# A four-layer convolution kernel: the deformable stage's preparation and tiles, ordered by image in place of by pair of images

## The reference, cut to what matters

```python
x = x + _L1_conv_ref(_gn(x), ...)    # 3x3 convolution, 64 to 64 channels, with bias
x = x + _L2_conv_ref(_gn(x), ...)    # deformable 3x3 convolution
# _gn: each of 32 groups (2 neighbouring channels of one image) to mean 0 and variance 1
# deformable: from the normed image, for each pixel and each of 9 taps,
off  = _conv(x, offset_w, offset_b)                   # a (dy, dx)
mask = 2.0 * sigmoid(_conv(x, mod_w, mod_b))
# the image at the displaced point, from its 4 corners, bilinearly; then
sampled = (v00*(1-wy)*(1-wx) + v01*(1-wy)*wx + v10*wy*(1-wx) + v11*wy*wx) * mask
out = einsum('bkhwc,ock->bohw', sampled, w2)
```

## Time and profile before

| what | value |
|---|---|
| median of three runs | 6821.06 us (6818.94 to 6823.68) |
| the profiled execution | 6821.58 us, span 6819.7 us |
| POOL busy | 4754.8 us, 70% of the span |
| DVE busy | 5149.9 us, 76% |
| PE busy | 4541.4 us, 67% |
| ACT busy | 2515.4 us, 37% |

### The profile page before, as it was taken

The page is one execution under the profiler, slowest core; times in us unless marked ns, Lnnn a source line. Parts: engine busy times, 40 slices in busy tenths (PEclk is TensorE's granted clock), DMA queues, the critical chain, the costliest instruction groups (busy, mean ns, idle before and its releaser), DMA issues. The chain is left out here.

```text
span 6819.7 us, 55261 instructions
## 1 busy us (share of the span) xinstructions
PE 4541.4 (67%) x14990; PEld 2454.8 (36%) x14990; DVE 5149.9 (76%) x4038; ACT 2515.4 (37%) x3865; POOL 4754.8 (70%) x3364
## 2 busy tenths in 40 slices
PE   2755765576466546633325787878888787888887
PEld 1543552233323323422222343434333343443443
DVE  2855864367666766766655898989989898998998
ACT  0111110212111101200005565666666565666664
POOL 0744752277777777777754787878878787887887
PEclk8766777575566566555557999999999999999999
DMA  3533542334443543433323444444454444444443
GB/s 115 115 73 67 115 92 63 94 104 122 124 130 104 142 131 104 136 120 105 105 87 113 147 152 142 153 139 162 141 151 149 145 148 150 150 152 142 153 151 117
DMA packets 377421, 853.16 MB, mean 125 GB/s; under 512 B 194816, under 2 KB 237720, under 8 KB 372772
## 3 DMA queue, kind: packets, MB, share of 16 engines
q1 hardware_dynamic: 292420, 618.02, 30.6%
q0 software_dynamic: 84672, 231.32, 11.2%
HBM read 766.90 MB, written 56.48 MB: 121 GB/s over the span
## 5 line engine op out<-in xcount | busy, mean ns | idle before, releaser
L2016 POOL TENSOR_TENSOR ma_hc<-ma_h,ma_cc 128x784 f32<-128x784 f32 x1024 | 1885.7, 1849 | 631.9 <-DVE ma_h L1918 497.6
L797 POOL DMA_INDIRECT fl_quad<-table,fl_idx x1764 | 1694.5, 961 | 779.0 <-issue 536.7
L1573 PE MATMUL ma_bank<-ma_hc,ident 128*128 128x392 f32 x4096 | 1530.1, 496 | 76.2 <-POOL ma_hc L2016 76.2
L1918 DVE TENSOR_TENSOR_SCAN ma_h<-ma_da,ma_state,ma_bank 128x784 f32<-128x784 f32 x768 | 1417.5, 1846 | 165.6 <-POOL ma_hc L2016 67.6
L1791 ACT ACTIVATE ma_da<-ma_dt,ma_a_neg 128x784 f32<-128x784 f32 x1024 | 948.3, 943 | 496.3 <-DVE ma_h L1918 479.5
L952 DVE TENSOR_TENSOR fl_part<-fl_quad,fl_bank 128x2304 f32<-128x2304 f32 x196 | 500.5, 2554 | 741.2 <-DMA fl_quad<-table,fl_idx 740.9
L1906 DVE TENSOR_TENSOR ma_bank<-ma_dtu,ma_bank 128x784 f32<-128x784 f32 x1024 | 981.3, 958 | 38.3 <-PE ma_bank L1560 37.6
L1094 PE MATMUL fl_bank<-ident,fl_tap 128*128 128x128 f32 (+1 forms) x980 | 245.8, 414 | 989.7 <-DVE xres L969 929.1
L1573 PEld LDWEIGHTS ma_bank<-ma_hc,ident 128*128 128x128 f32 x4096 | 711.1, 191 | 506.5 <-POOL ma_hc L2016 80.2
L1560 PE MATMUL ma_bank<-ma_bc,ma_sel 96*128 96x512 bf16 (+1 forms) x2048 | 518.9, 335 | 442.4 <-DVE ma_h L1918 430.9
L960 DVE TENSOR_REDUCE fl_tap<-fl_part 128x576 f32<-128x2304 f32 x196 | 796.4, 4063 | 0.1
(11 more groups left out here) (217 smaller groups left out, 6166.2 us busy)
## 6 DMA issues: line engine op xcount, KB each, us to landing
ma_cc<-c_rows SPq DMA_DIRECT2D x512, 784.0 KB, 4.1
mx_win<-flat SPq DMA_DIRECT2D x64, 878.0 KB, 10.4
fl_quad<-table,fl_idx POOLq DMA_INDIRECT x1764, 2.7
table<-fl_xt SPq DMA_DIRECT2D x64, 392.0 KB
mx_mask<-in_c_mask SPq DMA_DIRECT2D x56, 294.0 KB, 4.3
ma_xs<-ma_x SPq DMA_DIRECT2D x64, 196.8 KB, 5.4
ma_xs<-ma_x SPq DMA_DIRECT2D x64, 196.5 KB, 5.8
mx_xf<-flat SPq DMA_DIRECT2D x8, 816.0 KB, 15.1
```

Of the source, the lines that this page charges most:

```text
L797: gp.indirect_dma_start(quad[i][:, kk, :], None, k["tables"][q], bass.IndirectOffsetOnAxis(ap=idx[i][:, kk:kk + 1], axis=0))\
L1573: ins = pe.matmul(ps_y[:, t, :], ident[:], hc[:, n % RH, at], start=False, stop=(n == DS - 1))
L1918: dve.tensor_tensor_scan(h[:, i % RH, :], da[:, i % RH, :], ps_bu[i % 2], before, ALU.mult, ALU.add).then_inc(scand, 1)
L2016: gp.tensor_tensor(hc[:, i % RH, :], h[:, i % RH, :], cc[:, i % (NGRP * GRP), :], ALU.mult)\
```

## The change

Preparation is split by image. `program` begins with the first norm of pair 0 (`add_up`, 4 steps) and 24 steps of preparation of image 0; then come the tiles of image b, each followed by one step of image b + 1, and in steps 19 to 22 of an even image the first norm of the next pair. The tiles of a pair are no longer in alternation: 24 of image 0, 24 of image 1, the shared last one. Each image has a second norm of its own (`measure`, `variance`, `factors` with e = 1 + h), so a pair has three in place of two, each still over all 128 partitions. `y` gets a buffer of its own. POOL waits for one table at each image, and an even image's gathers get the first half of the table. SP stores the tables in the new order. Cut to its core, with the indices of semaphores left out where they only follow the new count:

```diff
-        def program(prepare, tile):
-            for s in range(NSEQ):
-                prepare(0, s)
-            for q in range(NPAIR):
-                for s in range(NSEQ):
-                    tile(q, s, NSEQ * q + s)
-                    if q + 1 < NPAIR:
-                        prepare(q + 1, s)
+        def program(add_up, prepare, tile):
+            for s in range(4):
+                add_up(0, s)
+            for s in range(NF):
+                prepare(0, 0, s)
+            for b in range(NB):
+                q, h = b // 2, b % 2
+                for s in range(NF + h):
+                    tile(NSEQ * q + NF * h + s)
+                    if s < NF and b + 1 < NB:
+                        prepare((b + 1) // 2, 1 - h, s)
+                    if h == 0 and 19 <= s < 23 and q + 1 < NPAIR:
+                        add_up(q + 1, s - 19)
...
-        y = om[:, 0:PIX]
+        y = s_.sb("y", [P, PIX])
...
             def load_y(q):
                 if q:
-                    sp.wait_ge(oturned, START + 4 * q)
+                    sp.wait_ge(joined, START + q)
...
             store_table(0)
-            store_table(1)
             for q in range(NPAIR):
                 if q + 1 < NPAIR:
-                    prepare(q + 1)
+                    load_y(q + 1)
+                store_table(2 * q + 1)
+                if q + 1 < NPAIR:
+                    store_table(2 * q + 2)
                 sp.wait_ge(added, START + NSEQ * (q + 1))
...
-                if s == 0:
+                if T == 0:
                     gp.wait_ge(bordered, START + 256 * NPAIR)
-                    gp.wait_ge(tabled, START + TABD * (2 * q + 2))
+                if s % NF == 0 and s < LAST:
+                    gp.wait_ge(tabled, START + TABD * (2 * q + s // NF + 1))
...
+                table = k["tables"][q][0:TAB, :] if s < NF else k["tables"][q]
                 for kk in range(K2):
-                    gp.indirect_dma_start(quad[i][:, kk, :], None, k["tables"][q],
+                    gp.indirect_dma_start(quad[i][:, kk, :], None, table,
...
+                if e == 2:
+                    dve.wait_ge(added, START + NSEQ * q + 8)
                 for i in range(NSTAT):
                     dve.bn_stats(stats[:, i, :], xres[:, q, i * STAT:(i + 1) * STAT]).then_inc(moments, 1)
...
+            def add_up(q, s):
+                if s == 0:
+                    join(q)
                 if s == 1:
-                    join(q)
+                    measure(q, 0)
                 if s == 2:
-                    measure(q, 0)
+                    variance(3 * q)
                 if s == 3:
-                    variance(2 * q)
-                if s == 4:
                     factors(q, 0)
...
+            def prepare(q, h, s):
+                b = 2 * q + h
+                if s == 0:
+                    pad(q, 0, h)
+                if 2 <= s <= 8:
+                    grow(q, h, s - 2)
+                if s == 8:
+                    measure(q, 1 + h)
+                if s == 9:
+                    variance(3 * q + 1 + h)
+                if s == 10:
+                    factors(q, 1 + h)
+                    pad(q, 1, h)
+                if s == 16:
+                    place(b, 0)
+                if s == 17:
+                    place(b, 1)
+                    corner(q, h)
+                if s == 18:
+                    weigh(q, h)
...
+            def prepare(q, h, s):
+                if 1 <= s <= 7:
+                    conv(q, h, s - 1)
+                if s == 8:
+                    pair(3 * q + 1 + h)
+                if 11 <= s <= 14:
+                    offset(q, h, 2 * (s - 11))
+                    if s < 14:
+                        offset(q, h, 2 * (s - 11) + 1)
+                if 15 <= s <= 18:
+                    turn_x(q, h, s - 15)
+                if 15 <= s <= 16:
+                    turn_offsets(q, h, s - 15)
...
+            def prepare(q, h, s):
+                if s == 0:
+                    pad(q, 0, h)
+                if s == 8:
+                    square(3 * q + 1 + h)
+                if s == 9:
+                    root(q, 1 + h)
+                if s == 10:
+                    pad(q, 1, h)
+                if 11 <= s <= 14:
+                    take_offsets(q, h, 2 * (s - 11))
+                    if s < 14:
+                        take_offsets(q, h, 2 * (s - 11) + 1)
+                if 15 <= s <= 18:
+                    take_x(q, h, s - 15)
+                if s == 17:
+                    sigmoid(2 * q + h)
```

More of the change, by code:

```diff
@@ L672, in stage_flow @@
         hd2, var, lnv = (s_.sb(x, [P, 1]) for x in ("hd2", "var", "lnv"))
-        rstd = [s_.sb(f"rstd{i}", [P, NPAIR]) for i in range(2)]
-        nmr = [s_.sb(f"nmr{i}", [P, NPAIR]) for i in range(2)]
+        rstd = [s_.sb(f"rstd{i}", [P, NPAIR]) for i in range(3)]
+        nmr = [s_.sb(f"nmr{i}", [P, NPAIR]) for i in range(3)]
         xp = s_.sb("xp", [P, PPIX])
         om = s_.sb("om", [P, PIX + HS])
-        y = om[:, 0:PIX]
+        y = s_.sb("y", [P, PIX])
         xt = s_.sb("xt", [2 * PW, NT, CH])
@@ L743, in store_table @@
                             sp.dma_start(dst, xt[yy * PW + 1:yy * PW + 1 + WW]).then_inc(tabled, 16)
[L745 to L748, removed]
             sp.wait_ge(cleared, START + 2)
@@ L811, in join, with measure @@
                 dve.wait_ge(y_in, START + 32 * (q + 1))
[L812 to L816, removed]
+                dve.tensor_tensor(xres[:, q, :], xres[:, q, :], y[:], ALU.add).then_inc(joined, 1)
+            def measure(q, e):
+                E = 3 * q + e
+                if e == 0:
                     dve.wait_ge(joined, START + q + 1)
                 else:
-                    dve.wait_ge(grown, START + 14 * (q + 1))
+                    dve.wait_ge(grown, START + 7 * (2 * q + e))
+                if e == 2:
+                    dve.wait_ge(added, START + NSEQ * q + 8)
                 for i in range(NSTAT):
                     dve.bn_stats(stats[:, i, :], xres[:, q, i * STAT:(i + 1) * STAT]).then_inc(moments, 1)
-                dve.wait_ge(moments, START + (NSTAT + 1) * e + NSTAT)
+                dve.wait_ge(moments, START + (NSTAT + 1) * E + NSTAT)
                 dve.bn_aggr(mv[:], stats[:]).then_inc(moments, 1)
@@ L828, in variance, with factors @@
                 dve.scalar_tensor_tensor(var[:], psn[:, 1:2], EPS, hd2[:], ALU.add, ALU.add).then_inc(varied, 1)
[L830 to L833, removed]
+            def factors(q, e):
+                E = 3 * q + e
+                dve.wait_ge(logged, START + 2 * E + 2)
+                dve.scalar_tensor_tensor(nmr[e][:, q:q + 1], psn[:, 0:1], -1.0, rstd[e][:, q:q + 1],
                                          ALU.mult, ALU.mult).then_inc(ready, 1)
-                dve.wait_ge(ready, START + e + 1)
+                dve.wait_ge(ready, START + E + 1)
             def pad(q, r, h):
                 own, rows = padded_rows(h)
-                dve.wait_ge(unread, START + 4 * q + 2 * r + h)
+                dve.wait_ge(unread, START + 4 * q + 2 * h + r)
                 dve.tensor_scalar(rows[0:CH, 1:1 + HH, 1:1 + WW],
                                   xres[own, q, :].rearrange("p (y x) -> p y x", y=HH),
-                                  rstd[r][own, q:q + 1], nmr[r][own, q:q + 1], ALU.mult, ALU.add).then_inc(padded, 1)
+                                  rstd[r * (h + 1)][own, q:q + 1], nmr[r * (h + 1)][own, q:q + 1],
+                                  ALU.mult, ALU.add).then_inc(padded, 1)
             def grow(q, h, c):
@@ L847, in grow @@
                 if c == 0:
-                    dve.wait_ge(shifted, START + 4 * q + h + 1)
+                    dve.wait_ge(shifted, START + 4 * q + 2 * h + 1)
                 x = xres[own, q, c * CCOL:(c + 1) * CCOL]
-                dve.scalar_tensor_tensor(x, cps[(7 * h + c) % 2][own, 0:CCOL], cbias[own, 0:1], x, ALU.add, ALU.add)\
+                dve.scalar_tensor_tensor(x, cps[c % 2][own, 0:CCOL], cbias[own, 0:1], x, ALU.add, ALU.add)\
                    .then_inc(grown, 1)
@@ L940, in pick @@
             def pick(T):
                 z = (T // NSEQ % 2) * NSEQ + T % NSEQ
-                if T % NSEQ == 0:
-                    dve.wait_ge(steps, START + NSTEP * (2 * (T // NSEQ) + 2))
+                s = T % NSEQ
+                if s % NF == 0 and s < LAST:
+                    dve.wait_ge(steps, START + NSTEP * (2 * (T // NSEQ) + s // NF + 1))
                 dve.tensor_copy(idx[T % RQ][:], idx_all[:, z, :]).then_inc(picked, 1)
@@ L966, in add @@
                 if s < LAST:
-                    own = slice((s % 2) * CH, (s % 2 + 1) * CH)
-                    x = xres[own, q, (s // 2) * TS:(s // 2 + 1) * TS]
+                    h, t = divmod(s, NF)
+                    own = slice(h * CH, (h + 1) * CH)
+                    x = xres[own, q, t * TS:(t + 1) * TS]
                     dve.tensor_tensor(x, ops[own, :], x, ALU.add).then_inc(added, 1)
@@ L975, in add, with tile @@
```

(58 more changed lines are left out.)

60 lines of the change are left out of this document (14 added, 46 removed).

## The result

| | before | after |
|---|---|---|
| median (range) | 6822.37 us (6818.94 to 6824.74, 4 runs) | 6738.98 us (6731.52 to 6740.77, 4 runs) |
| profiled execution, span | 6821.58 us, 6819.7 us | 6738.43 us, 6736.6 us |
| POOL idle before the first gather | 241.9 us | 155.8 us |
| first to last gather | 2230.6 us | 2234.4 us |

The ratio is 0.9876, 95% interval [0.9859, 0.9893]: 83.4 us less, where 83.8 had been forecast; the time lies 1.7 us above the forecast and inside the range.

The account below looks back on a forecast made before the run. POOL's pace was taken to bound 196 tiles behind a serial head. An earlier first gather (-86.8 us) and lengthened gathers (+3.0) gave -83.8, laid on the median 6821.06: 6737.3 us, range 6724 to 6759.

Parts of the forecast that it names:

- POOL's pace bounds the tiles, so the head is what counts: Gather stage: a serial head, then 196 tiles at POOL's pace; the first gather comes 86.8 us earlier, at 1213.1.
- The same chain behind image 0: Head: last `grow` to last copy 51.33 us plus 0.3, now behind image 0; table store to first gather 21.75.
- that rival: Offset convolution in the head at 2.4 GHz instead of 1.2: 12.5 us less, time 6725; chance 0.07.
- An image more beside the gathers: Beside tiles: seven images prepared beside gathers instead of six, lengthening POOL's gathers by 3.0 us.
- The bound of 14.0 us: Upper bound for the added image beside gathers: each of its DVE instructions holds POOL for its length; sum 6748.
- No new wait at the images: POOL's waits for the tables of images 1 to 7: tables in time by 17 us, price 0.
- L: Time from an image's last copy into `xt` to its landed table, read as 27.6 us beside gathers.
- A third `measure`, the separate `y`, the sliced table: Beside tiles: one more `measure` per pair hidden in DVE's free time, separate buffer and sliced table; price 0.

Follow-up runs that it names:

- e1: Changed kernel with both images of the first pair prepared before the first tile; ratio to the kernel before 0.9992, median 6821.35 us.
- e4: Changed kernel with the pads of images 1 to 7 done by ACT in place of DVE; ratio to the kernel before 0.9845, median 6721.3 us.
- e2: Changed kernel with turns and copies into `xt` of images 1 to 7 two steps later; 6766.76 us, one run.
- e3: Changed kernel with turns and copies into `xt` of images 1 to 7 three steps later; 6804.1 us, one run.

## Why the prediction was right

1. *POOL's pace bounds the tiles, so the head is what counts.* Right. Of the span's 83.1 us, 0.7 were already won when image 0's last `grow` ended: POOL's last instruction ahead of the stage ends at 1057.0 in place of 1058.0, in a part without edits. From there to the first gather it was 160.2 us and is 73.7: 86.5 less, 86.8 forecast. (Before, POOL's idle time had one more exception than the prediction counted, 0.3 us put down to DVE's picks; nothing hangs on it.) e1 gives the head back and the gain with it.
2. *The same chain behind image 0.* The last `grow` to the last copy took 51.46 us (51.6 forecast, with 0.3 for the order of the turns), store to gather 22.25 (21.75). The offsets kept the low clock, 0.50 granted, so that rival did not occur; how the clock is granted was not tried.
3. *An image more beside the gathers.* Right in kind, a little small: 3.8 us from first to last gather where the step had 3.0. The gathers lengthened at pads make up 18.3 us in 14 (e4 removes them), where the kernel before had 14.5 us in 12. In the row above the gather began 0.62 us after the pad did, and ended 0.82 us after the pad's end: it is held until the pad is over, so its price depends on where in the pad it begins. Taking one image as half of a pair's average carried over the old places: at the new ones the three joins lengthen gathers by 6.6 us in place of 8.8, and the row numbers and weights by 5.2 in place of 3.1. That these two shifts nearly cancel is luck. The other DVE instructions of an image add little, as the prediction took from the sum of the rows: the 5.2 us are those of seven images. The bound of 14.0 us, every DVE instruction at full length, is far from the 3.8. The Trainium skill (SBUF — State Buffer, "SBUF: two separate sides") has the shared port pair as an exclusive lock, which some DVE operations take and others do not, and says that ACT never waits for anyone. The trace agrees: DVE's pads hold gathers and its `measure` does not the earlier trace rows, and ACT's pad takes 3.00 us beside gathers (e4) as in the head without them.
4. *No new wait at the images.* Right: none of 1763. The margin was read as 17 us; with L at 26.2 and the store 47.0 us ahead, it is 21 at image 1. e2 and e3 show that it is a margin and not the absence of a dependence: two steps later the waits are there.
5. *A third `measure`, the separate `y`, the sliced table.* At nothing, as forecast; no gather beyond the ones at pads, joins, corners and weights is lengthened by more than 40 ns, the first aside.

## What to carry to other kernels

In a pipeline whose steady state is bound by one engine, count the serial part ahead of that engine's first instruction: cutting the unit of preparation in half is worth what it takes off there (86.5 us here), less what the moved work does to the bounding engine's own instructions (3.8 us). Before moving work so, measure the margin of each new wait in units of the bounding engine's step, since beyond the margin a step of slip costs nearly a step per boundary: at image 1 the third step raised the wait from 3.99 to 13.31 us, of a tile's 11.25. Then look at what else stands between: here a store that could run beside the rest of the head, and DVE instructions that hold the engine of the gathers and that ACT did here without a new wait.

## What the runs showed of the hardware that was not expected

A gather beside DVE's pad is lengthened by anything from 1.0 us to 1.6 us with the same pad, by its place alone (1946 to 2581 ns for the 14 in the kernel after). A table store of 12,656 packets needs 26.2 us to be usable beside running gathers, 24.1 us when POOL pauses, 21.75 to 22.25 us alone: gathers and store share the DMA engines at a loss of a fifth for the store and of nothing for POOL, whose gathers beside a store keep their median of 0.95 us with 0.30 between them. The median gather was 946 ns in most executions, 949 in those of e2 and e4; the cause is open.
